# Cross attention and routed experts on one core: bias on TensorE, masked copies on ACT, moved side work, and zeroed rows by expert

## What is computed

```python
x = x + attention(layernorm(x), ctx, mask, mask)     # x: 8 x 256 x 512
x = x + experts(layernorm(x))                        # 2048 tokens of 512

def attention(target, source, target_mask, source_mask):   # 16 heads of 16
    q = Wq @ target + bq; k = Wk @ source + bk; v = Wv @ source + bv
    dot = q.T @ k / 4
    mask = target_mask[..., None] * source_mask[..., None, :]
    amap = softmax(mask * dot - (1 - mask) * 1e6) * mask
    return amap @ v

def experts(h):                                      # 8 experts, top 2, inner width 352
    w, sel = top_k(softmax(h @ gate.T), 2)
    return sum over both of w / sum(w) * (silu(g) * u) @ w2[sel].T    # g, u = h @ w1[sel].T
```

## Time and profile before

| what | value |
|---|---|
| median of 3 runs | 883.87 us |
| lowest, highest | 882.66, 886.34 us |
| the profiled execution | 884.46 us, of which its span is 882.7 |
| mean granted clock of TensorE | 0.972 |
| busy: TensorE, its weight loads | 806.0, 365.6 us |
| busy: VectorE, ACT, POOL | 557.7, 322.9, 371.7 us |

### The profile page before, as it was taken

One profiled execution on the slowest core, in us unless ns is written; L12 is line 12 of the kernel. 1 busy time (PEld: TensorE's weight loads), 2 busy tenths in 40 slices (PEclk: granted clock), 3 DMA queues, 4 the chain that ended last, 5 costly groups with the idle time before them and its releaser, 6 DMA issues. The chain is left out here.

```text
span 882.7 us, 12845 instructions
## 1 busy us (share of the span) xinstructions
PE 806.0 (91%) x3757; PEld 365.6 (41%) x3758; DVE 557.7 (63%) x1071; ACT 322.9 (37%) x619; POOL 371.7 (42%) x392
## 2 busy tenths in 40 slices
PE   4888898989999998999999998999799999999993
PEld 2332332333333332333333332466466656655661
DVE  5678887888888888788787875345333333333331
ACT  0035455555555655655655657521000000000000
POOL 7544264556655755755755423333122212211221
PEclk9579999999999999999999999999999999999998
DMA  5744567666765865855745532355447555464332
GB/s 176 235 130 137 175 185 233 205 211 194 236 199 176 261 191 171 254 156 174 240 138 158 170 111 85 107 127 129 120 72 205 141 138 149 73 165 71 60 61 34
DMA packets 84524, 138.02 MB, mean 156 GB/s; under 512 B 14765, under 2 KB 40685, under 8 KB 84474
## 3 DMA queue, kind: packets, MB, share of 16 engines
q1 hardware_dynamic: 68970, 108.65, 41.3%
q0 software_dynamic: 7744, 17.86, 10.6%
q10 hardware_dynamic: 7760, 10.89, 4.3%
HBM read 77.36 MB, written 59.36 MB: 155 GB/s over the span
## 5 line engine op out<-in xcount | busy, mean ns | idle before, releaser
L837 ACT ACTIVATE pr<-sc 128x512 f32<-128x512 f32 x512 | 269.9, 601 | 220.3 <-PE sc L1500 217.7
L982 DVE TENSOR_REDUCE mx<-tile 128x2 f32<-128x1024 f32 x256 | 308.2, 1215 | 63.3 <-PE tile L1512 55.8
L1512 PE MATMUL tile<-qk 97*128 97x512 bf16 x496 | 150.7, 388 | 28.0 <-DVE mx L982 21.5
L1500 PE MATMUL sc<-qk 100*128 100x512 bf16 x512 | 155.1, 384 | 9.1 <-DMA qk<-mxt 6.2
L759 POOL DMA_INDIRECT out_dram<-xin,ids x36 | 56.3, 1565 | 228.9 <-DVE ids L1305 224.7
L1538 PE MATMUL pvb<-pr,vp 128*32 128x512 f32 x1024 | 138.1, 612 | 0.0
L1512 PEld LDWEIGHTS tile<-qk 97*128 97x128 bf16 x496 | 34.6, 97 | 163.8 <-DVE mx L982 85.5
L1653 PE MATMUL pvb<-wring,qkf 128*128 (+1 forms) x216 | 98.7, 593 | 1.6 <-DVE qkf L1315 1.6
L1632 PE MATMUL sc<-wring,xh 128*128 x288 | 92.9, 466 | 0.0
L1632 PE MATMUL tile<-wring,xh 128*128 x288 | 91.3, 460 | 0.0
L714 POOL TENSOR_SCALAR parts<-qkf 128x512 bf16<-128x512 f32 x31 | 46.7, 1505 | 103.4 <-DVE qkf L1066 98.7
(11 more groups left out here) (158 smaller groups left out, 793.0 us busy)
## 6 DMA issues: line engine op xcount, KB each, us to landing
qk<-stack_d SPq DMA_DIRECT2D x32, 768.0 KB
stack_d<-parts SPq DMA_DIRECT2D x32, 384.0 KB, 2.8
wring<-w_dram SPq DMA_DIRECT2D x32, 352.0 KB, 7.1
cin<-routed_d ACTq DMA_DIRECT2D x36, 257.0 KB, 2.8
stack_d<-parts SPq DMA_DIRECT2D x32, 256.0 KB, 3.1
pv_d<-ov SPq DMA_DIRECT2D x32, 256.0 KB, 3.9
xin<-x_dram SPq DMA_DIRECT2D x16, 256.0 KB, 5.4
cin<-ctxt_dram SPq DMA_DIRECT2D x8, 512.0 KB, 6.3
```

Source lines behind the costliest of these rows:

```text
L837: nc.scalar.activation(pr[s % 2][:, j, :], sc[(32 * u + 4 * s + j) % NSC][:, :], ACT.Exp, scale=SCALE).then_inc(exped.sem, 1)
L982: dve.tensor_reduce(cols, t[:, :, :], X, ALU.max, negate=True).then_inc(drained.sem, 1)
L1500: nc.tensor.matmul(sc[(32 * u + 4 * s + j) % NSC][:, :], ks[half(u)][0:ALL_ROWS, h, c * P:c * P + P], qs[half(u)][0:ALL_ROWS, h, :], start ...
L1512: last = nc.tensor.matmul(t[:, i, :], qs[half(w)][0:RAW_ROWS, h, c * P:c * P + P], ks[half(w)][0:RAW_ROWS, h, :], start=True, stop=True)
```

## The change

It has five parts.

Values: the bias is added on TensorE by a bf16 matmul of four rows in front of each of the four column groups. The rows are the three bf16 parts of the bias, prepared by nine small operations on POOL (`bias_parts`) once at the start. ACT copies the four groups out of PSUM with the mask as its scale, straight into `vp`; the operations of VectorE and POOL go. The values move from step 1 to step 0 in all units but the first. In the starting sequence they now wait for `bias_made` and `const_made`, and the first ACT operation is a copy instead of an exponential.

Tokens: VectorE writes one normalized copy, ACT makes the second (`token_twin`) in step 3. `choose` reads the logits in PSUM and leaves their copy out.

Order: transposes of tokens and logits move one step ahead (3 and 4). On VectorE the batch statistics move behind the maxima 14 and 15, the normalization into the next unit, and the choice ahead of maximum 14. POOL takes the batch's reciprocal root after the residual. In each step three scores stand ahead of the raw scores instead of two.

Zero rows: each zero block has its own semaphore; SP, when all eight are issued, waits for them in turn and counts them in `pads_in`. ACT reads the row and expert of a tile first and then waits for the count of its expert. Three operations of the plan move ahead of the end of the row table.

```diff
-        return (["v"] if s == 1 ...) + (["q"] if s == 3 ...) + (["xT"] if s == 4 ...) + (["logits"] if s == 5 ...)
+        return (["v"] if s == VALUES_AT[n > 0] ...) + (["q"] if s == 3 ...) + (["xT"] if s == 3 ...) + (["logits"] if s == 4 ...)
...
# SP
             for e in range(E):
                 row = sp.value_load(padrow[0:1, e:e + 1], min_val=e * CAP, max_val=e * CAP + TOKENS)
-                sp.dma_start(routed_d[bass.ds(row, P), :], pad[:, :]).then_inc(padded, 16)
+                sp.dma_start(routed_d[bass.ds(row, P), :], pad[:, :]).then_inc(pad_in[e], 16)
+            for e in range(E):
+                sp.wait_ge(pad_in[e], 16)
+                sp.sem_inc(pads_in, 1)
             for e in range(WRING):
                 sp.wait_ge(weights_in[e], 16 * CHUNKS)
                 sp.sem_inc(experts_in, 1)
...
# POOL
+                b = bv_s[0:4, :]
+                do(pool.tensor_scalar(bvb[:, 0, :], b, 1.0, None, ALU.mult))
+                do(pool.tensor_tensor(bvr[:, 0, :], b, bvb[:, 0, :], ALU.subtract))
+                do(pool.tensor_scalar(bvb[:, 1, :], bvr[:, 0, :], 1.0, None, ALU.mult))
+                do(pool.tensor_tensor(bvb[:, 2, :], bvr[:, 0, :], bvb[:, 1, :], ALU.subtract))
+                for i in range(3):
+                    do(pool.tensor_scalar(bvp[:, i, :], bvb[:, i, :], idf[0:4, i:i + 1], None, ALU.mult))
+                do(pool.tensor_tensor(bvb[:, 0, :], bvp[:, 0, :], bvp[:, 1, :], ALU.add))
+                do(pool.tensor_tensor(bvb[:, 1, :], bvb[:, 0, :], bvp[:, 2, :], ALU.add))
...
             part(-3, 0)
+            pool.wait_ge(const_loaded, CONST)
+            bias_parts()
             part(-2, 0)
             part(-1, 1)
-            values_out(-1)
...
-                if has(u + 5):
-                    batch_rstd(u)
                 if has(u + 3):
                     part(u, 0)
                 if has(u - 1):
                     residual(u)
+                if has(u + 5):
+                    batch_rstd(u)
...
# ACT
+            def values_out(u):
+                w = u + 1
+                act.wait_ge(ready.sem, ready.at(u, "v"))
+                if (due := pved.at(u - 1, 7)) is not None:
+                    act.wait_ge(pved.sem, due)
+                t = tiles[slot_no(u, "v")]
+                for c in range(4):
+                    nc.scalar.activation(vp[half(w)][:, c, :, 0:D],
+                                         t[:, 0, c * P:c * P + P].rearrange("p (h d) -> p h d", d=D),
+                                         ACT.Copy, scale=mc[:, batch(w), c:c + 1]).then_inc(vmade.sem, 1)
+
+            def token_twin(u):
+                act.wait_ge(normed2.sem, normed2.at(u, "n"))
+                nc.scalar.activation(xa[:, half(u), 1, 0:T], xa[:, half(u), 0, 0:T], ACT.Copy
+                                     ).then_inc(twin.sem, 1)
...
-                        if (s, j) == (5, 0) and has(u - 2):
+                        if (s, j) == (1, 0 if u else 3) and has(u + 1):
+                            values_out(u)
+                        if (s, j) == (3, 1) and has(u - 2):
+                            token_twin(u)
+                        if (s, j) == (4, 0) and has(u - 2):
                             transposed_out(u)
...
             def load(n, k):
+                row = entry(act, ROWS, n, E * CAP + 3 * P)
+                if later(n, EARLY):
+                    expert = entry(act, EXPERT, n, E - 1)
+                    act.wait_ge(pads_in, expert + 1)
                 act.wait_ge(xt_made, n - 1)
-                row = entry(act, ROWS, n, E * CAP + 3 * P)
                 act.dma_start(xl[:, k, :], routed_d[bass.ds(row, P), :]).then_inc(xl_in[k], 16)
...
             act.wait_ge(routed.sem, routed.total())
-            act.wait_ge(padded, 16 * (E + 5))
...
# VectorE
             def unit(u):
                 maximum(u, u + 1, 4)
+                normalize(u - 1)
                 maximum(u, u + 1, 5)
...
-                values_out(u)
...
                 maximum(u, u + 1, 10)
-                batch_stats(u, 0)
                 reciprocals(u, 0)
                 maximum(u, u + 1, 11)
-                batch_stats(u, 1)
                 reciprocals(u, 1)
                 projection_out(u, 0)
 
                 maximum(u, u + 1, 12)
                 maximum(u, u + 1, 13)
-
-                maximum(u, u + 1, 14)
-                normalize(u)
-                maximum(u, u + 1, 15)
                 choose(u, 0)
                 choose(u, 1)
                 choose(u, 2)
                 choose(u, 3)
 
-                maximum(u, u + 2, 0)
+                maximum(u, u + 1, 14)
+                batch_stats(u, 0)
+                maximum(u, u + 1, 15)
+                batch_stats(u, 1)
                 choose(u, 4)
-                maximum(u, u + 2, 1)
                 choose(u, 5)
-                split_maxima(u, u + 1, ALL)
...
+                maximum(u, u + 2, 0)
+                maximum(u, u + 2, 1)
+                split_maxima(u, u + 1, ALL)
...
# TensorE
                 for s in range(4):
+                    nc.tensor.matmul(t[:, 0, s * P:s * P + P], ones[0:4, :],
+                                     bvb[:, 1, half(w) * P:half(w) * P + P], start=True, stop=False)
                     for c in range(2):
...
                         scores(u, s, 0)
                         scores(u, s, 1)
+                    if has(u):
+                        scores(u, s, 2)
                     for w, m in todo[:1]:
                         raw_scores(u, w, m)
                     if has(u):
-                        scores(u, s, 2)
                         scores(u, s, 3)
```

More of the change, by code:

```diff
@@ L121, in fillers @@
 def fillers(n, s):
-    return ((["v"] if s == 1 and has(n + 1) else []) + (["q"] if s == 3 and has(n + 3) else [])
-            + (["xT"] if s == 4 and has(n - 2) else []) + (["logits"] if s == 5 and has(n - 2) else []))
+    return ((["v"] if s == VALUES_AT[n > 0] and has(n + 1) else []) + (["q"] if s == 3 and has(n + 3) else [])
+            + (["xT"] if s == 3 and has(n - 2) else []) + (["logits"] if s == 4 and has(n - 2) else []))
 def tile_events(n):
@@ L323, in attention @@
         plan_made = sem("plan_made")
+        pad_in = [sem(f"pad_in{e}") for e in range(E)]
+        pads_in = sem("pads_in")
         passed = sem("passed")
@@ L338, in attention @@
         ready = Count(sem("tile_ready"), TILES)
-        drained = Count(sem("tile_drained"), [t for t in TILES if t[1] != "xT"])
+        drained = Count(sem("tile_drained"), [t for t in TILES if t[1] not in ("xT", "v")])
         xt_out = Count(sem("xt_out"), of(-2, "xT"))
@@ L649, in ones_of, with bias_parts, do @@
                 pool.wait_ge(ones_made, 2 * h + 2)
-            def values_out(u):
-                w = u + 1
-                pool.wait_ge(const_loaded, CONST)
-                pool.wait_ge(drained.sem, drained.at(u, "v"))
-                if (due := pved.at(u - 1, 7)) is not None:
-                    pool.wait_ge(pved.sem, due)
-                pool.tensor_tensor(vp[half(w)][:, :, :, 0:D],
-                                   vt[:, :, :].rearrange("p c (h d) -> p c h d", d=D),
-                                   mc[:, batch(w), :].rearrange("p (c a b) -> p c a b", a=1, b=1)
-                                   .broadcast_to([P, 4, UH, D]), ALU.mult).then_inc(vmade.sem, 1)
+            def bias_parts():
+                at = [0]
+                def do(ins):
+                    at[0] += 1
+                    ins.then_inc(bias_made, 1)
+                    pool.wait_ge(bias_made, at[0])
+                b = bv_s[0:4, :]
[7 more added lines that the diff above has]
+                do(pool.tensor_tensor(bvb[:, 1, :], bvb[:, 0, :], bvp[:, 2, :], ALU.add))
+                assert at[0] == BIAS_MADE
             def scatter(u):
@@ L733, in residual @@
                     pool.wait_ge(x1_kept.sem, due)
-                if (due := normed2.at(u - 1, 1)) is not None:
+                if (due := normed2.at(u - 1, "n")) is not None:
                     pool.wait_ge(normed2.sem, due)
@@ L933, in token_normalize @@
                 dve.wait_ge(rstd2.sem, rstd2.at(u, "pow"))
-                if j == 0 and (due := routed.at(u - 1, 1)) is not None:
+                if (due := routed.at(u - 1, 1)) is not None:
                     dve.wait_ge(routed.sem, due)
-                dve.tensor_scalar(xa[:, half(v), j, 0:T], x1[:, half(v), :], l2[:, 6:7], l2[:, 8:9],
+                dve.tensor_scalar(xa[:, half(v), 0, 0:T], x1[:, half(v), :], l2[:, 6:7], l2[:, 8:9],
                                   ALU.subtract, ALU.mult).then_inc(normed2.sem, 1)
@@ L1069, in projection_out @@
                     op0=ALU.add, op1=ALU.mult).then_inc(drained.sem, 1)
-            def values_out(u):
-                w = u + 1
-                if not has(w):
-                    return
-                t = tile_of(u, "v")
-                if (due := vmade.at(u - 1, "v")) is not None:
-                    dve.wait_ge(vmade.sem, due)
```

(12 more changed lines are left out.)

74 lines of the change are left out of this document (36 added, 38 removed).

## The result

The changed kernel takes 893.51 us against 884.23 of the kernel before in the same session, a ratio of 1.0105 with a 95% interval of 1.0063 to 1.0148. It is slower by 1%, where 874.5 us (864 to 884) was forecast. The profiled execution has a span of 890.3 us, 7.6 more than that of before.

The account below looks back on a forecast made before the run. TensorE bounds the kernel, waiting for VectorE in each attention unit's second half and for the ninth tile's rows. From 883.87 us: -5.9 zeroed rows, -2.8 eleven units, -1.5 first units, +0.8 start, giving 874.5 (864 to 884).

Parts of the forecast that it names:

- Zeroed rows: Gap before the ninth tile's matmuls: fetch waits only for its expert's zero block, 4.2 us, full clock 1.7; together 5.9 gained.
- Rival (d): Zero blocks hold the ninth tile's fetch as before, since SP counts late or the expert is late: 880 us, chance 0.07.
- Values: Attention units: four bf16 bias matmuls of four rows cost TensorE 0.3 us a unit, bounds 0 and 0.48.
- What would show it: List of trace signs for the forecast, among them values taking 2.2 us of TensorE and units of 31.6 us.
- ACT's copies: Step 1 of a unit: four copies delay ACT's exponentials by 1.0 us, of which 0.3 reach TensorE, bounds 0 and 0.8.
- Order: Rearranged TensorE and VectorE work in attention units: unit of 30.9 us, 0.9 less, if nothing blocks VectorE.
- Three scores first: nothing more: Attention steps: putting a third score ahead of the raw scores gains nothing more, but passes ACT's delay on.
- Blocked operations: VectorE's compare and sum, held by POOL's operations in their new place, cost 0.7 us a unit: 31.6, gain 0.25.
- rival (c): Slower: compare and sum both caught in nearly every unit, 2.3 us instead of 0.7; 894 us, or 888 with 1.8; chance 0.14.
- rival (a): VectorE is rarely blocked: 30.9 us a unit, -10 instead of -2.8, so 867 us; chance 0.22.
- Start and first units: Table load with ACT's first copy costs 0.8 us at the start; units 0 to 2 win 1.5 in all.
- rival (b): Attention gives nothing because ACT's stall and the blocks eat all of it: 879 us, chance 0.18.

## Why the prediction was wrong

**Zeroed rows: right, a little large.** Forecast 5.9. The wait fell from 4.45 to 1.45 and the clock's 1.7 came back: 3.0 and 1.7, of which the stretches of the table show 3.0 and 1.4, in the changed kernel, and the run with this part alone 4.9. What was missed are the two terms of the landing time, 9.7 for the issues and 3.7 for the fetch. In the changed kernel the fetch took 5.1; in the one with this part alone it took 3.5, and the issues 10.6. The fetch now flies beside the last blocks, and whether that is what lengthens it is not shown. SP counts behind its eighth issue, as said. Rival (d) is out.

**Values: this step failed.** "I take 0.3" with bounds of 0 and 0.48 a unit became 1.31 in the values and 1.40 in the unit's length, with little less in the first units. I had priced a matmul of 4 rows from the pitch of 128-row matmuls in the same tile (0.12 in the earlier trace rows), by its columns, and asked only what could hide it. The trace of before had that very change, in rows that I did not read: the ranks' first matmul has one row, and the next starts 0.11 or 0.10 behind it, where the third, of 128 rows like the second, follows after 0.04 (TensorE's timeline, kernel before):

```profile
285.39 0.17 PE L1599 MATMUL tile<-first,ones 1*128 1x8 bf16 x1
285.49 0.18 PE L1600 MATMUL tile<-selb,upper 128*128 128x8 bf16 x1
285.53 0.17 PE L1601 MATMUL tile<-before,ones 128*128 128x8 bf16 x1
```

Padded to 128 rows, or four in a row, the bias matmuls add 0.44 to the values, which take 2.2 us, the number of "What would show it". With the four in a row the kernel stands at 0.9959 x 883.87 = 880.3. Of the 18.7 us between the forecast and 1.0105 x 883.87 = 893.2, this term is 15: 12.9 by the kernel that only puts the four in a row, and 0.13 x 16 = 2.1 by which even those are above 0.3. The kernel without them gives 21.6 - 0.3 x 16 = 16.8 by its ratio.

**ACT's copies: right.** Four copies delay the exponentials so that the raw scores of step 2 start 0.95 us behind its three scores, where they start 0.65 behind in other steps: 0.30, as forecast. VectorE's lost addition and ACT's second token copy show in no wait of TensorE, as said.

**Order: right in sum, in part by luck.** Without the bias' 0.3 the forecast had 0.55 a unit for order and blocks together. In units 3 to 12 of the changed kernel the bias costs 14.0 and the ten units are 7.3 longer, so 6.7, or 0.67 a unit, were won. Errors offset each other. "Three scores first: nothing more" is worth 0.3 a unit. Against it, VectorE's wait of 0.34 to 0.37 stays, where I had taken all of VectorE's waits as gone. A unit without bias and blocks was to be 30.6 and is 30.77 at its shortest, and the blocks cost less than the 0.7 that I took.

**Blocked operations: mechanism right, size nearly.** Forecast 0.7 a unit, from seven in eleven compares by 0.6 and one sum in five. In the changed kernel six of the ten units from 3 to 12 wait 1.0 with the maxima's transpose and are 0.8 longer, 0.5 on average, in three of them by a compare of 1.14 to 1.25 beside GpSimd's multiply, in three by a sum of 1.14 to 1.20. Where the compare is caught, the sum slips in before GpSimd's next operation (0.17 at 416.26, GpSimd at 416.27), so the two are never both caught in one unit, which takes the ground from rival (c): the kernel is slower, but not by its mechanism. Moving both gave 6 to 8 us. That is rival (a)'s mechanism, VectorE hardly blocked, though not its 30.9 and 867: with the bias in one matmul and the move the units are 31.28, and the kernel measures 0.9883, 873.5.

**Start and first units.** Forecast +0.8 and -1.5. With the table load ahead of ACT's first copy, the first raw scores wait 2.47. Unit 0's k projection is 1.7 later, 0.9 with the four bias matmuls in a row. Units 1 and 2 together are 0.2 shorter, 2.0 with those in a row. So both terms fit once the bias is cheap, but no closer than about 1 us: with one bias matmul, as cheap, the same two stretches are 1.7 longer and 1.6 shorter. GpSimd's nine bias operations took 8.2 us (7.7 said) and nothing behind them is seen to wait for them.

**Units 13 to 15 and the first tiles** are 3.3 longer, and but for unit 13's 0.25 I had given them nothing. Two units' biases lie in that stretch (2 x 1.40 = 2.8), and the first tile waits 1.2 more for its rows (2.54, not 1.35). But with the bias matmuls in a row it is still 3.8 longer than before, with one bias matmul 1.3, and with compare and sum moved as well 0.1. Between the first two of these lie that DMA wait (2.45 and 1.34) and the clock: from the first tile's transposes to the second's it is 10.2 us at a granted clock of 0.83 in the kernel before, the changed one and the one with four in a row, and 9.0 at 1.00 in the two with one bias matmul. What sets the DMA wait, and why the clock differs there, stays open, and so does the blocking's share.

Added up for the kernel with its bias matmuls in a row, 880.3 against 874.5: the zeroed rows are short by 1.0 and the bias by 2.1; the rest, 2.7, is no more than its stretch from unit 12 to the eighth tile shows. That account is rough, since the profiled execution took 882.28 us and the median is 877.78. Its time is that of rival (b), attention that gives nothing, but not for (b)'s reasons: the blocks cost less than forecast.

## What to carry to other kernels

Before you put a small matmul between large ones, look at the rows of the stationary tile as well as at its columns. A matmul on another share of the array costs on the way there and on the way back; pad it to the full rows with zeros, or put all of its kind in one place. And when an experiment confirms a theory, ask which other thing its edit changed too: grouping the matmuls fitted a change of type exactly, until a run changed only the rows. An operation that another engine can block belongs where that engine is idle by the trace, even if it must stand earlier than its result is needed.

## What the runs showed of the hardware

- Going from matmuls of 128 rows to 4 or 64 and back costs TensorE 0.24 us (0.80 a turn, against 0.56 with 128 rows): 0.10 on the way there (0.54 against 0.44 at the first bias) and so 0.14 on the way back. From 97 rows to 128 and from 128 to 100 no step shows. The records of the large matmuls behind it grow from 0.66 to 0.71 for four, so part of the price is booked on instructions that did not change.
- Going from scores to four products side by side in the array, of 32 columns each, takes 0.31 us from start to start instead of 0.22, in both kernels.
- The change between bf16 and fp32 is cheap: four 128-row bias matmuls among the pairs take 2.22 with the values, one of the same columns ahead of them 2.00, so each further matmul with its change there and back adds 0.07.
- A one-row fp32 matmul of 128 columns adds 0.61 us at such a place, against the 0.35 of the 4-row bf16 one.
- A blocked compare ends 0.03 us behind GpSimd's multiply (416.22 and 416.19), and the sum behind it starts 0.01 before GpSimd's add and is not blocked. So it is in the unit shown and, to 0.01 us, in every unit of these traces with a blocked compare of this order.
